# Attention products by query on 32 rows of the array, without key blocks, and identity products before the products by key

## The chip, the cores and the metric

The kernel runs on one core of a Trainium2 chip. The metric is the device time of one execution in microseconds (us), median over the runs.

## What is computed

64 sequences (B) of 128 tokens (S), width 128 (D), attend to 120 context rows each (KL) with 16 heads of 8, and a mixture of 8 experts with two experts per token follows. Both parts add to x.

```
x = x + xattn(layernorm(x), ctx, ctx, mask, Wq, bq, Wk, bk, Wv, bv, Wo, bo)
x = x + ffn(layernorm(x), Wr, W1, b1, W2, b2)

xattn:  score = einsum('bhqd,bhkd->bhqk', q, k) / sqrt(8)
        score = where(mask, -1e30, score)
        out   = softmax(score) @ v, heads joined, @ Wo + bo
ffn:    probs = softmax(x @ Wr.T); the two largest of 8 weigh
        gelu(x @ W1[e] + b1[e]) @ W2[e] + b2[e]
```

## The kernel before

It is one program with a stream written out by hand for each engine: SP and ACT issue DMAs, GpSimd (POOL) scatters rows, PE is TensorE, DVE is VectorE. Semaphores join them. The attention part works on chunks of two sequences (32 chunks) and is unrolled in slots: in `slot(n)` every engine does its share of several chunks at once, chunk n in the products by key, chunks n+1 and n+2 in the products by query, chunk n+3 in the projections, chunks n-1 to n-4 in what follows. All engines' `slot` functions list their steps in a fixed order, and so each engine works strictly in that order. The expert part (the loop `tiles`) begins after the last slot, at some 480 us.

Queries and keys are projected (L1189, L1190), split into a high and a low part in the type fp32r (L1012, L1013, L684), and spread by DMA from `comp` to `dense[c % 4]` (L292 to L302). A dense row has 128 partitions: four groups j of 32 rows, one for each of four heads, and along the free axis four groups g, each with 256 query columns (two sequences) and 240 key columns. Rows of a group of 32 that hold no part of a head carry constants: in the query columns the row MSK is one, so that a mask row in the key operand adds the mask to the score; the rows NHI and NLO take minus the largest score of each query.

The scores are computed twice:

- By query (`by_query`, L1249): the stationary operand is 128 query columns of dense with all 128 rows, the moving operand is a block-diagonal copy of the keys, `kb[c % 2]`, with 4 heads x 120 keys = 480 columns. One product gives the scores of four heads for 128 queries. DVE takes the maximum over the keys (`best`, L695). There are eight such products in a chunk, into two banks of PSUM (`wide`) in turn. The maxima are transposed (`turn_maxima`, L1287), negated and split (L702, L704), and written by DMA into the rows NHI and NLO of the query blocks (`maxima`, L327).
- By key (`by_key`, L1261): the stationary operand is 120 key columns of dense, the moving operand the block-diagonal copy of the queries `qb[c % 2]`, 4 x 128 = 512 columns. The exponential (ACT, L997) reads it from two banks (`scores`) in turn, with the mask as a bias of each key (`mcol`). Then follow the 16 products with the values (`weigh`, L1276), on all rows and 32 columns of the array each; the heads are copied (L1029) and transposed (L1216), divided (L668), transposed (L1229) and projected (L1237).

The block-diagonal copies are DMAs of four blocks each: `query_blocks` (L319) on SP's queue, a slot ahead of their use, and `key_blocks` (L1069) on ACT's queue, after the exponentials of t = 0 and 1 in the slot and ahead of `take_heads`, `take_rows` and `take_x`. `key_blocks` waits until the dense rows have landed (`dn_in`). `mask_rows` (L309) on SP writes the mask row of kb and waits for the first of the key blocks (`kfirst`). Both copies lie in memory that is cleared once at the start: kb by DVE (L878, L908), qb by ACT (`clear`). The expert part reuses kb and qb for weights.

## Time and profile before

| | us |
|---|---|
| median of 3 runs | 844.66 |
| lowest, highest | 834.1, 855.23 |
| the profiled execution | 847.77 |
| its span in the profile | 846.0 |
| attention part, first to last transposed maxima | 33.8 to 447.8 |

The profiled execution's time is 1.8 us above its span, for what lies around it. Busy times say how long an engine had an instruction in work; matmuls overlap each other, so on PE the chain of waits tells better what each adds. "issue" is time in which the profile shows nothing that was waited for.

### The profile page before, as it was taken

What the parts mean: (1) busy time and instruction counts of PE and PEld (TensorE: products, weight loads), DVE (VectorE), ACT (ScalarE), POOL (GpSimd) and SP (SyncE); (2) the same over time, 40 slices, a digit from 0 to 9 for tenths busy, and PEclk for the clock granted to TensorE, in tenths of its full rate; (3) what the DMA queues carried; (4) which work ended last, traced back from release to release, by engine and by line L of the source; (5) the groups of instructions that cost most, each with busy time, mean ns of one, the idle gap of its engine ahead of it and who ended that gap; (6) DMA issues with size and microseconds to landing.
All of it is one profiled execution on the core that took longest, in us unless ns stands there. A gap on an engine that the chain in (4) does not pass through costs nothing.

```text
span 846.0 us, 18252 instructions
## 1 busy us (share of the span) xinstructions
PE 658.2 (78%) x4964; PEld 494.5 (58%) x4964; DVE 554.3 (66%) x1813; ACT 528.3 (62%) x1060; POOL 492.4 (58%) x892
## 2 busy tenths in 40 slices
PE   1787888878888988888888376998888898988500
PEld 0455666656566666666565255876776686766400
DVE  4556778867877778687875454666555565646436
ACT  3466776856776767667776265877666676858300
POOL 8233376665757666676768642675654565665710
PEclk9879999989998999999999578999999999999855
DMA  4756667666766576566751368876666756664069
GB/s 139 211 165 188 209 209 238 187 186 191 231 193 190 190 229 209 171 204 179 222 167 61 94 217 258 253 234 196 205 195 192 220 181 195 215 207 132 10 243 352
DMA packets 118905, 164.24 MB, mean 194 GB/s; under 512 B 22479, under 2 KB 77286, under 8 KB 118823
## 3 DMA queue, kind: packets, MB, share of 16 engines
q1 hardware_dynamic: 88711, 126.14, 48.3%
q10 hardware_dynamic: 21024, 20.06, 8.3%
q0 software_dynamic: 9088, 17.07, 6.4%
q8 instruction: 36, 0.59, 0.3%
q14 instruction: 46, 0.38, 0.1%
HBM read 73.07 MB, written 33.92 MB: 126 GB/s over the span
## 4 chain that ended last, share of the span: by engine, by line
PE 53%; issue 13%; ACT 8%; DMA 7%; POOL 6%; ACTq 6%; DVE 4%; SPq 2%; another core or an unknown queue 1%; POOLq 0%; DVEq 0%
ACTq L1069 5%; PE bank L1261 5%; PE bank L1249 4%; PE bank L1276 4%; PE bank L1429 4%; PE bank L1427 4%; PE bank L1428 4%; PE bank L1412 3%; PE bank L1415 3%; PE bank L1413 3%; DMA qb<-yd 3%; PE bank L1189 3%; PE bank L1216 2%; ACT pt L997 2%; POOL xd L538 2%
## 5 line engine op out<-in xcount | busy, mean ns | idle before, releaser
L638 POOL DMA_INDIRECT yd<-vs,idt x156 | 159.5, 1022 | 129.4 <-DVE vs L949 84.5
L538 POOL DMA_INDIRECT xd<-rows,posi x128 | 128.9, 1007 | 104.9 <-DVE posi L800 75.2
L935 DVE TENSOR_TENSOR qb<-hid,qb 128x512 fp32r<-128x512 f32 x156 | 108.3, 694 | 105.6 <-ACT hid L1143 68.4
L695 DVE TENSOR_REDUCE mx<-bank 128x4 f32<-128x480 f32 x256 | 159.7, 649 | 26.4 <-PE bank L1249 19.6
L997 ACT ACTIVATE pt<-bank,mcol 120x512 f32<-120x512 f32 x256 | 168.5, 692 | 10.2 <-PE bank L1261 10.1
L1140 ACT ACTIVATE qb<-bank,btile 128x512 fp32r<-128x512 f32 x156 | 109.1, 699 | 80.1 <-PE bank L1429 55.7
L1261 PE MATMUL bank<-qb,dense 128*120 128x512 f32 x256 | 103.6, 470 | 11.6 <-issue 4.5
L1143 ACT ACTIVATE hid<-bank,btile 128x512 f32<-128x512 f32 x156 | 108.8, 697 | 0.0
L1029 ACT ACTIVATE ots<-bank 128x512 f32<-128x512 f32 x64 | 38.2, 598 | 102.5 <-PE bank L1276 36.8
L1249 PE MATMUL bank<-kb,dense 128*128 128x480 f32 x256 | 88.8, 428 | 7.2 <-DVE mx L695 3.4
L1276 PE MATMUL bank<-pt,vs 120*32 120x128 f32 x2048 | 72.8, 282 | 1.5 <-issue 1.4
L1276 PEld LDWEIGHTS bank<-pt,vs 120*32 120x32 f32 x2048 | 54.1, 112 | 23.5 <-issue 16.3
L1249 PEld LDWEIGHTS bank<-kb,dense 128*128 128x128 f32 x256 | 46.4, 201 | 27.6 <-DVE mx L695 10.0
L1261 PEld LDWEIGHTS bank<-qb,dense 128*120 128x120 f32 x256 | 42.4, 195 | 25.2 <-issue 13.4
L665 DVE RECIPROCAL rden<-bank 128x16 f32<-128x16 f32 x64 | 16.2, 254 | 48.7 <-PE bank L1216 48.5
L1216 PE MATMUL bank<-ident,ots 128*128 128x128 f32 x256 | 43.9, 299 | 2.9 <-ACT x2s L1077 2.9
L1427 PE MATMUL bank<-kb 128*128 128x512 f32 x80 | 33.8, 422 | 10.3 <-issue 6.9
L548 POOL TENSOR_TENSOR y<-ve,minus_half 128x4 f32<-128x4 f32 x38 | 39.6, 1042 | 3.2
L1427 PE MATMUL bank<-kb,qb 128*128 128x512 f32 x76 | 32.5, 427 | 11.3 <-DVE kb L901 11.3
L1216 PEld LDWEIGHTS bank<-ident,ots 128*128 128x128 f32 x256 | 35.2, 163 | 7.3 <-ACT ots L1029 3.6
L1229 PE MATMUL bank<-ident,on 128*128 128x128 f32 x64 | 19.1, 299 | 24.4 <-ACT xT L1003 19.2
L1412 PE MATMUL bank<-qb 128*128 128x512 f32 x76 | 34.7, 457 | 2.2 <-ACT qb L1140 2.2
(169 smaller groups left out, 1559.7 us busy)
## 6 DMA issues: line engine op xcount, KB each, us to landing
kb<-wd SPq DMA_DIRECT2D x40, 512.0 KB
qb<-wd SPq DMA_DIRECT2D x38, 512.0 KB
qb<-dense SPq DMA_DIRECT2D x128, 128.0 KB
dense<-comp SPq DMA_DIRECT2D x64, 248.0 KB
kb<-dense ACTq DMA_DIRECT2D x128, 120.0 KB
rows<-xd SPq DMA_DIRECT2D x39, 264.0 KB
wd<-wsp SPq DMA_DIRECT2D x16, 512.0 KB
qb<-yd SPq DMA_DIRECT2D x16, 512.0 KB, 6.0
```

Of the source, the lines that this page charges most:

```text
L538: g.indirect_dma_start(xd, bass.IndirectOffsetOnAxis(ap=posi[r % 4][:, bk:bk + 1], axis=0), rows[r % 4][:, bk // 2, bk % 2, :], None, boun ...
L638: g.indirect_dma_start(yd, bass.IndirectOffsetOnAxis(ap=idt[k][:, j:j + 1], axis=0), yrow[p.parity][:, j, :], None, bounds_check=2 * NTOK ...
L695: v.tensor_reduce(mx[c % 2][:, :, gg, b], wide[m % 2][:, 0:J * KL].rearrange("p (j k) -> p j k", j=J), op=ALU.max, axis=AX.X).then_inc(w_f ...
L935: v.tensor_tensor(hhl[:, 1, c, :], hid[:, c % 2, :], hhl[:, 0, c, :], ALU.subtract).then_inc(h_lo, 1)
L997: a.activation(pt[i % NP][:].rearrange("p j q -> p (j q)"), scores[t % 2][0:KL, :], ACT.Exp, bias=mcol[:, 2 * c + t // G:2 * c + t // G + ...
L1140: a.activation(hhl[:, 0, c, :], bank[c][:, :], ACT.Gelu, bias=bias).then_inc(h_hi, 1)
L1143: a.activation(hid[:, c % 2, :], bank[c][:, :], ACT.Gelu, bias=bias).then_inc(h_val, 1)
L1216: last = t_.transpose(small[0][:, g * P:(g + 1) * P], ots[w % 2][:, g, :], ident[:, :])
L1249: t_.matmul(wide[m % 2][:, 0:J * KL].rearrange("p (j k) -> p j k", j=J), dense[c % ND][:, g, b * S:(b + 1) * S], kb[c % 2][:, :, g, b * KL ...
L1261: t_.matmul(scores[t % 2][0:KL, :].rearrange("p (j q) -> p j q", j=J), dense[c % ND][:, g, N2 + b * KL:N2 + (b + 1) * KL], qb[c % 2][:, :, ...
L1276: last = t_.matmul(heads[R * j:R * j + R, g * S:(g + 1) * S], vs[c % 2][:, b, G * g + j, :], pt[(4 * w + g) % NP][:, j, :], start=True, st ...
L1427: t_.matmul(bank[c][:, :], w[:, 0, 0, cs], xh, start=True, stop=False)
```

## The change

- `kb`, `key_blocks`, its semaphores and its clearing are gone. `by_query` takes both operands straight from dense: for each head group j a product on the 32 rows of j, 128 query columns stationary and 120 key columns moving. 32 products a chunk stand for eight. They come in four groups of eight: two values of j in turn, each with its own bank, for the four g. A group waits until both banks are free and signals each bank at its last product.
- A bank now holds the four g of one j (it held the four j of one g); `best` writes the maxima accordingly.
- The mask row goes into the key columns of dense (`mask_rows`), in all four groups of 32 rows; it is in both products now, so the exponential has no bias and the transposed mask isn't loaded. The constant rows are set up by other values of MSK, NLO, NHI.
- `qb` has three buffers and not two. `query_blocks` is issued one slot earlier and now waits for `dn_in` itself; `mask_rows` stands ahead of it.
- Ahead of every even product by key there is a product of the identity with itself, plain fp32, 256 columns, into the first bank of `scores`, which the product by key then overwrites.
- The expert part's four weight tiles lie in qb[1] and qb[2]; the split x has a buffer of its own.

```diff
-        NHI, NLO, MSK = 3, 7, 11
+        MSK, NLO, NHI = 11, 15, 31
...
             def mask_rows(c):
+                if c < ND:
+                    sp.wait_ge(dense_set, 2 * (c + 1))
+                else:
+                    sp.wait_ge(b_full, 8 * (c - ND + 1))
                 if c == 0:
                     sp.wait_ge(mask_dram, 16)
-                sp.wait_ge(kfirst[c % 2], 16 * (c // 2 + 1))
-                sp.dma_start(kb[c % 2][MSK:MSK + 1]...
+                sp.dma_start(dense[c % ND][MSK::R, :, N2:NK]...
...
             def query_blocks(c):
-                if c < 2:
-                    sp.wait_ge(qb_zero, c + 1)
+                if c < NB:
+                    sp.wait_ge(qb_zero[c], 1)
                 else:
-                    sp.wait_ge(b_full, 8 * (c - 1))
+                    sp.wait_ge(b_full, 8 * (c - NB + 1))
+                sp.wait_ge(dn_in[c % 2], 64 * (c // 2 + 1))
...
             def slot(n):
-                if chunk(n + 1):
-                    query_blocks(n + 1)
+                if chunk(n + 3):
+                    mask_rows(n + 3)
                 if chunk(n + 2):
-                    mask_rows(n + 2)
+                    query_blocks(n + 2)
...
-                v.tensor_reduce(mx[c % 2][:, :, gg, b], wide[m % 2][:, 0:J * KL].rearrange("p (j k) -> p j k", j=J),
+                v.tensor_reduce(mx[c % 2][:, j, :, b], wide[m % 2][:, 0:G * KL].rearrange("p (g k) -> p g k", g=G),
...
-            v.memset(flat(kb[0], "p j g n").bitcast(F32), 0.0).then_inc(kb_zero, 1)
+            v.memset(flat(qb[2], "p j g n").bitcast(F32), 0.0).then_inc(qb_zero[2], 1)
...
-                if n == -3:
-                    v.memset(flat(kb[1], "p j g n").bitcast(F32), 0.0).then_inc(kb_zero, 1)
...
-                a.activation(pt[i % NP][:].rearrange("p j q -> p (j q)"), scores[t % 2][0:KL, :], ACT.Exp,
-                             bias=mcol[:, 2 * c + t // G:2 * c + t // G + 1], scale=SCALE).then_inc(exp_done, 1)
+                a.activation(pt[i % NP][:].rearrange("p j q -> p (j q)"), scores[t % 2][0:KL, :], ACT.Exp, scale=SCALE).then_inc(exp_done, 1)
...
-            def key_blocks(c):
-
-                if c < 2:
-                    act.wait_ge(kb_zero, c + 1)
-                else:
-                    act.wait_ge(w_full, 8 * (c - 1))
-                act.wait_ge(dn_in[c % 2], 64 * (c // 2 + 1))
-                for j in range(J):
-                    act.dma_start(kb[c % 2][R * j:R * j + R, j, :, :].bitcast(F32),
-                                 dense[c % ND][R * j:R * j + R, :, N2:NK].bitcast(F32)).then_inc((kblk if j else kfirst)[c % 2], 16)
...
-            def by_query(c, u):
+            def by_query(c, p):
...
-                b, g = divmod(u, G)
-                if u == 0:
-                    pe.wait_ge(kblk[c % 2], 48 * (c // 2 + 1))
-                    pe.wait_ge(mask_row[c % 2], 16 * (c // 2 + 1))
-                m = 8 * c + u
-                if m >= 2:
-                    pe.wait_ge(w_free, m - 1)
-                t_.matmul(wide[m % 2][:, 0:J * KL].rearrange("p (j k) -> p j k", j=J), dense[c % ND][:, g, b * S:(b + 1) * S],
-                          kb[c % 2][:, :, g, b * KL:(b + 1) * KL], start=True, stop=True).then_inc(w_full, 1)
+                b, half = divmod(p, 2)
+                if p == 0:
+                    pe.wait_ge(dn_in[c % 2], 64 * (c // 2 + 1))
+                    pe.wait_ge(mask_row[c % ND], 16 * (c // ND + 1))
+                m = 8 * c + 2 * p
+                if m:
+                    pe.wait_ge(w_free, m)
+                for g in range(G):
+                    for k in range(2):
+                        j = 2 * half + k
+                        last = t_.matmul(wide[k][:, g * KL:(g + 1) * KL], dense[c % ND][R * j:R * j + R, g, b * S:(b + 1) * S],
+                                         dense[c % ND][R * j:R * j + R, g, N2 + b * KL:N2 + (b + 1) * KL], start=True, stop=True, tile_position=(R * j, 0))
+                        if g == G - 1:
+                            last.then_inc(w_full, 1)
...
             def by_key(c, t):
...
+                if t % 2 == 0:
+                    t_.matmul(scores[0][:, 0:2 * P].rearrange("p (a n) -> p a n", a=2), ident[:, :],
+                              ident[:, :].rearrange("p (a n) -> p a n", a=1).to_broadcast([P, 2, P]), start=True, stop=True)
```

On PE, around the first products by key of a slot in the middle of the attention part, the order before is this (each row is an instruction with what it writes and reads; L1261 by key, L1249 by query, L1276 with the values, L1237 the output projection):

```order
L1309 MATMUL bank<-wrT,x2s 128x8 x2
L1216 MATMUL bank<-ident,ots 128x128 x4
L1261 MATMUL bank<-qb,dense 120x512 x2
L1237 MATMUL bank<-wraw,onT 128x128
L1249 MATMUL bank<-kb,dense 128x480 x2
L1276 MATMUL bank<-pt,vs 32x128 x16
```

and after the change (L1252 is the identity product, L1254 by key, L1237 by query, L1221 the projection, L1269 with the values):

```order
L1302 MATMUL bank<-wrT,x2s 128x8 x2
L1200 MATMUL bank<-ident,ots 128x128 x4
L1252 MATMUL bank<-ident 128x256
L1254 MATMUL bank<-qb,dense 120x512 x2
L1221 MATMUL bank<-wraw,onT 128x128
L1237 MATMUL bank<-dense 128x120 x8
L1269 MATMUL bank<-pt,vs 32x128 x16
```

Nothing has changed places; one instruction is added and two have become eight.

On ACT, at the beginning of a slot, the order before is this (L997 exponentials, L1059 of the router, L1029 the heads, L1077 and L1003 what PE transposed):

```order
L997 ACTIVATE pt<-bank,mcol 120x512
L1059 ACTIVATE tope<-topd 128x16
L997 ACTIVATE pt<-bank,mcol 120x512
L1069 DMA kb<-dense 32x4x240 x4
L1029 ACTIVATE ots<-bank 128x512
L1077 ACTIVATE x2s<-bank 128x256
L1003 ACTIVATE xT<-bank 128x256
```

and after the change:

```order
L995 ACTIVATE pt<-bank 120x512
L1056 ACTIVATE tope<-topd 128x16
L995 ACTIVATE pt<-bank 120x512
L1026 ACTIVATE ots<-bank 128x512
L1063 ACTIVATE x2s<-bank 128x256
L1000 ACTIVATE xT<-bank 128x256
```

The four DMA issues are gone from between the exponential and the heads.

On SP, a slot before the change (L319 query blocks, L309 mask row, L292 to L302 dense rows, L327 maxima):

```order
L319 DMA qb<-dense 32x4x256 x4
L309 DMA kb<-maskd 1x16x240
L292 DMA dense<-comp 32x4x256
L294 DMA dense<-comp 32x4x240
L327 DMA qb<-negm 1x32x128 x2
L300 DMA dense<-comp 32x4x496
L302 DMA dense<-comp 32x4x496
```

and after it:

```order
L309 DMA dense<-maskd 4x4x240
L320 DMA qb<-dense 32x4x256 x4
L289 DMA dense<-comp 32x4x256
L291 DMA dense<-comp 32x4x240
L328 DMA qb<-negm 1x32x128 x2
L297 DMA dense<-comp 32x4x496
L299 DMA dense<-comp 32x4x496
```

The mask row has moved ahead of the query blocks, and both now belong to the chunk after the one they served before.

## Rows read from the trace of the kernel before

**Rows 1.** The page, part 1: busy us, share of the span, instructions

```profile
PE 658.2 (78%) x4964; PEld 494.5 (58%) x4964; DVE 554.3 (66%) x1813; ACT 528.3 (62%) x1060; POOL 492.4 (58%) x892
```

**Rows 2.** The line L1287: ns least/median/most, first and last start in us

```profile
L1287 PE MATMUL bank<-ident,mx x32: 270/273/421, 33.8 to 447.8; 128*32 128x128 f32 x32
```

**Rows 3.** Busy us of each engine between 60 and 450 us

```profile
core 0: us, PE busy (x) PEld busy (x) DVE busy (x) ACT busy (x) POOL busy (x), PEclk, DMA share, GB/s
60.00:450.00 390.00, 334.56 (x3373) 242.22 (x3372) 299.88 (x1283) 274.86 (x626) 247.86 (x505) 0.96 0.66 196
```

**Rows 4.** The chain of waits, 236 to 268 us: start us, length us, what

```profile
239.53 0.41 PE bank L1309 x4
...
252.74 1.90 issue
254.64 0.72 PE bank L1261 x2
255.37 0.22 PE bank L1237 x2
255.59 0.43 PE bank L1249 x2
256.02 1.64 PE bank L1276 x32
...
260.62 0.60 PE bank L1189 x2
261.22 0.41 PE bank L1190 x2
...
262.07 0.46 PE bank L1261 x2
...
263.07 1.01 PE bank L1276 x32
...
264.50 0.44 PE bank L1201 x4
...
266.10 0.49 PE bank L1309 x4
266.59 0.49 PE bank L1216 x4
...
267.14 0.84 PE bank L1261 x2
```

**Rows 5.** The chain between 60 and 450 us: shares by line, longest pieces

```profile
by line: issue 13.0%; PE bank L1261 10.7%; ACTq L1069 10.2%; PE bank L1276 9.4%; PE bank L1249 8.6%; PE bank L1216 5.1%; ACT pt L997 4.9%; PE bank L1189 4.5%; PE bank L1237 4.1%; PE bank L1190 3.3%; PE bank L1201 3.0%; ACT xn L1043 2.6%; DM
...
132.59 5.05 DMA kb<-dense
146.88 4.75 DMA kb<-dense
```

**Rows 6.** Instructions of ACT in order of time, 225 to 232 us

```profile
227.43 3.27 ACTq L1069 DMA_DIRECT2D kb<-dense  x3
230.80 0.60 ACT L1029 ACTIVATE ots<-bank 128x512 f32<-128x512 f32 x1 [3.12 <-issue]
```

**Rows 7.** The line L1069: ns least/median/most, first and last start

```profile
L1069 ACTq DMA_DIRECT2D kb<-dense x128: 592/632/1714, 18.8 to 433.4; - x128
```

**Rows 8.** Groups between 60 and 450 us: busy us, mean ns, idle before

```profile
L695 DVE TENSOR_REDUCE mx<-bank 128x4 f32<-128x480 f32 x232 | 145.1, 648 | 21.3 <-PE bank L1249 14.5 <-issue 5.7 <-remote 0.5
...
L1249 PEld LDWEIGHTS bank<-kb,dense 128*128 128x128 f32 x232 | 40.3, 194 | 19.6 <-DMA kb<-dense 5.6 <-issue 3.8 <-DVE mx L695 3.7
...
L1309 PEld LDWEIGHTS bank<-wrT,x2s 128*128 128x128 f32 x108 | 14.1, 190 | 0.9
```

**Rows 9.** PE's waits between 60 and 450 us: total, times, longest

```profile
PE bank L1229 <- ACT xT L1003: 17.2, 15, 1.9
...
PE bank L1229 <- issue: 4.1, 6, 1.1
```

**Rows 10.** The chain of waits, 10 to 24 us

```profile
16.25 3.26 DVE kb L908
...
19.54 0.62 ACTq L1069
```

More of the change, by code:

```diff
@@ L90, in moe_attention @@
         dense = [sb(f"dense{k}", [P, G, NK], F32R) for k in range(ND)]
-        qb = [sb(f"qb{k}", [P, J, G, N2], F32R) for k in range(2)]
-        kb = [sb(f"kb{k}", [P, J, G, K2], F32R) for k in range(2)]
+        qb = [sb(f"qb{k}", [P, J, G, N2], F32R) for k in range(NB)]
         vs_all = [sb(f"vs{k}", [P, 2, H, R]) for k in range(2)]
@@ L104, in moe_attention @@
         bias_qk = sb("bias_qk", [P, 2])
-        ones_k = sb("ones_k", [P, 1])
+        pad_q = sb("pad_q", [P, 1])
+        pad_k = [sb(f"pad_k{i}", [P, 1]) for i in range(3)]
         masku = sb("masku", [B, KL], mask.dtype)
@@ L201, in moe_attention @@
         w_in, w_in2, wqk_in, bias_in = (sem(k) for k in ("w_in", "w_in2", "wqk_in", "bias_in"))
-        dense_set, kb_zero, qb_zero, pad_set = sem("dense_set"), sem("kb_zero"), sem("qb_zero"), sem("pad_set")
+        dense_set, qb_zero, pad_set = sem("dense_set"), [sem(f"qb_zero{k}") for k in range(NB)], sem("pad_set")
         x_in, ctx_in = four("x_in"), [sem(f"ctx_in{k}") for k in range(NC)]
-        mask_in, mask_f, mask_dram, mcol_done = sem("mask_in"), sem("mask_f"), sem("mask_dram"), sem("mcol_done")
-        mask_row = two("mask_row")
+        mask_in, mask_f, mask_dram = sem("mask_in"), sem("mask_f"), sem("mask_dram")
+        mask_row = four("mask_row")
         ident_done, bo_done, half_done, vs_zero = sem("ident_done"), sem("bo_done"), sem("half_done"), sem("vs_zero")
@@ L211, in moe_attention @@
         w_full, w_free = sem("w_full"), sem("w_free")
-        dn_in, qblk, kblk, kfirst, mrow = two("dn_in"), two("qblk"), two("kblk"), two("kfirst"), two("mrow")
+        dn_in, qblk, mrow = two("dn_in"), [sem(f"qblk{k}") for k in range(NB)], two("mrow")
         v_full, v_taken = sem("v_full"), sem("v_taken")
@@ L977, in _, with clear @@
             a = nc.scalar
[L980 to L981 removed]
+            def clear(k):
+                a.activation(flat(qb[k], "p j g n"), ident[:, P - 1:P].to_broadcast([P, J * G * N2]), ACT.Copy, scale=0.0).then_inc(qb_zero[k], 1)
             for k, w in ((0, Wq), (1, Wk)):
```

68 lines of the change are left out of this document (28 added, 40 removed).

## The prediction

> **What bounds the kernel now.** I read the busy times first [rows 1]: no engine is full (PE 78%, DVE 66%, ACT 62%), and the matmul part, the first 450 us, differs from the expert part behind it, so I cut there. Of the change, everything lies in the attention part. The transposes of the maxima (L1287, one in a slot) start at 33.8 us for the first chunk and at 447.8 us for the last [rows 2]: 31 slots in 414 us, 13.36 us each. That period is what the change can move. In it PE is busy 334.6 us of 390, DVE 299.9, ACT 274.9, at a granted clock of 0.96 [rows 3].
>
> A busy PE says little, since records of matmuls overlap. What an instruction really adds is in the chain of waits, where each has only its own step [rows 4]. At full clock: two products by key 0.46 us, two by query 0.43, the 16 value products (32 records) 1.01, a pair of 128-column plain fp32 records 0.22, and so on. A slot holds four pairs by key (1.84), four by query (1.74), twice the value products (2.02), twice L1216 (0.93) and L1237 (0.44), and once L1189 and L1190 (0.84 without the start in L1189's 0.60), L1201 (0.44) and L1309 (0.45). The small ones, L1296, L1175, L1229, L1287 and L1319 to L1322, come to some 0.9 us at the 0.11 us a record that L1216 and L1237 show. Together that is 9.6 us of PE work. The other 3.8 us are waits and the slower pace behind them: in [rows 4] the chain stands 1.90 us before L1261, and the value products after it take 1.64 us and not 1.01.
>
> What PE waits for is in the chain's shares [rows 5]. ACTq L1069 has 10.2% of 390 us, 39.8 us or 1.36 us in a slot: the four DMA issues of the key blocks hold the ACT queue, and heads, rows and xT, which PE waits for, stand behind them. The timeline shows it [rows 6]: three of the issues from 227.43 to 230.70, and ots (L1029) only at 230.80 after 3.12 us of idle ACT. Two landings of key blocks, 5.05 and 4.75 us, are the longest pieces there [rows 5], another 0.34 us in a slot.
>
> **The change part by part.** (1) Key blocks go. Their 128 issues of 0.63 us [rows 7] leave ACT's queue: 2.5 us in a slot. ACT's busy 274.9 us over 29.2 slots is 9.4 us, with the issues 11.9, just under a short slot, as the 12.5 us from 254.64 to 267.14 in [rows 4]; without them 9.4. I take 1.36 + 0.34 = 1.7 us off the period. The 15.7 MB that they moved also go; I price that at nothing, since the landings that I have counted are their own, and it can only shorten the wait for qb<-negm.
>
> (2) Products by query. Eight of 480 columns (0.43 us a pair, 1.74 us in all) become 32 of 120 columns on 32 rows, still with 128 stationary columns each. No row shows such a product, so I bound it. From below: 216 ns for 480 columns is 54 ns for 120, and no more if everything but the columns hides: 1.7 us, no change. From above, where the load sets the pace: L1309 streams only 8 columns behind a 128-column load and takes 0.41 to 0.49 us for four records, 0.103 to 0.122 us each [rows 4]: 3.3 to 3.9 us. Its load lasts 190 ns, that of L1249 194 ns [rows 8], so the load of the fp32r operand is of the same kind. Beyond that, if a short fp32r product streamed like plain fp32: L1190 takes 0.41 us for two records of 240 columns, so 0.205 us for 120 columns: 6.6 us. The nearest row for products on part of the array is L1276: 32 records of 128 columns in 1.01 us, 32 ns each, where L1237 takes 110 ns for a record of as many columns; there four positions of the array overlap 3.5 times. The new products alternate between two positions of rows (two banks). If both load and stream overlapped the pace would be 0.103/2 = 0.052, if nothing did 0.103. I take 0.07: 2.24 us, that is +0.5 us in a slot.
>
> A rule speaks against this. The Trainium skill, page "TensorE: Matmul & The Clock Gate", section "LDWEIGHTS (loading the stationary operand)", says that a load costs by its columns and not by its rows, 32x128 as much as 128x128, and gives 107 ns by its formula. By that the 32 loads would be an estimated 3.4 us and the slot 1.2 us longer than with my value. L1309's 0.103 agrees with the figure; that fewer rows don't help is shown by no row here. The skill's page "TensorEngine Tiling (Array Packing)", section "Key Properties", says that different tiles can load and multiply in parallel, which is the lower end, but also that a change of tiling mode drains the engine; the kernel would then pay eight more such changes in a slot, which no row here prices.
>
> (3) Identity products. Four in a slot, plain fp32, 256 columns, into the first bank of scores ahead of every even product by key. L1190, the same type with 240 columns, takes 0.41 us, so 256 take 0.43 (L1189's 0.60 has a start in it): 4 x 0.43 = 1.72 us. They wait for what the product by key behind them waits for, so they can't fill its wait; they stand before it on PE, and the exponential behind them starts 0.43 us later.
>
> (4) Waits and queues. A group of eight products now needs both banks of wide free, and gives both at its end; the two maxima (648 ns each [rows 8]) then run one after the other. The next group is over 2 us away, and DVE has 299.9/29.2 = 10.3 us of work in a slot, so I price this at nothing; were the cover gone, it would be one maximum, 0.65 us, in each of four groups. On SP the mask rows and the query blocks come a slot earlier and now wait for the landing of the dense rows; behind them stand the loads and the dense rows of the next chunk. Before, SP waited there for kfirst, a landing after that of the dense rows, so nothing is later.
>
> (5) Hidden part. Of the 3.8 us, 2.1 remain after (1). Some of these are waits that more PE work covers: the last DMA of maxima, and L1229's wait for xT, 17.2 + 4.1 us in the window [rows 9], 0.73 a slot. I let 0.7 us be hidden.
>
> (6) Start. One 3.26 us memset of kb stands in the chain at 16.25 us and three issues of 0.62 behind it [rows 10]; the other memset becomes one of qb, 0.2 us longer. 3.26 + 1.86 - 0.2 = 4.9, say -5 us.
>
> Sum: 13.36 - 1.7 + 0.5 + 1.72 - 0.7 = 13.2 us, 0.2 less than before. Over 31 slots -6, with the start -11. The expert part, its weight tiles now in qb, stays. From the profiled execution's 847.8 us this gives 837. The median of the three runs is 844.7, 3 us lower, inside their own spread of 834 to 855, so I leave it at 837.
>
> **The rivals.**
> A. The two positions overlap fully and PE's waits close further: 54 ns, +0.0 for (2), 1.0 hidden. 13.36 - 1.7 + 1.72 - 1.0 = 12.4 us, -30 and -5: 813 us. For it: L1276's overlap, and the short slots of 12.5 us, in which ACT was nearly full. Against it: 120 columns are too few to cover a load, and 32 positions of columns are not positions of rows.
> B. Loads set the pace, the slower side. Place: the 32 products by query on PE; price 0.103 to 0.122 us each, +1.6 to +2.1 us in a slot for (2). 13.36 - 1.7 + 1.72 + 1.6 - 0.7 = 14.3, +28 - 5: 870 us, and 886 with 0.122. It decides from 0.095 us per product on. For it: L1309. Against it: 8 columns are not alternating rows.
> C. Short fp32r products run as plain fp32 without overlap: 0.205 each, +4.8 in a slot, 17.8 us with 0.4 hidden: 980 us. For it only the bound.
> D. The waits are replaced by others and nothing is hidden (the waits called issue have 13.0% of the chain [rows 5] and I can't name them): 13.36 - 1.7 + 0.5 + 1.72 = 13.9, +16 - 5: 859 us, no measurable change.
> A clock that falls, because the products on 32 rows or the idle time count for less, would show as B does, with a lower granted clock; the identity products stand against it, and 0.96 now says there is little to gain.
>
> **How the numbers follow.** Forecast 0.33 (its own range 826 to 850), A 0.28, D 0.10, B 0.23, C 0.06. Below 808 I see nothing; of B's tail and C some 0.09 lies above 885: range 808 to 885. Faster by over 2%, below 828, is A and a little of the forecast: 0.34. Slower by over 2%, above 862, is B and C and the edge of D: 0.30. Within 2%, about what this kernel's measurement can tell from nothing: 0.36.
>
> **What would show it.** Right: no ACTq time in the chain; ots right behind the exponential; eight products by query in the chain at about 0.56 us; identity pairs at 0.43; L1280 (the maxima's transposes) 13.2 us apart; the first one before 29 us. Eight products at 0.85 us or more are B, at 1.6 C, at 0.43 A. I am wrong in the waits if PE idle per slot stays over 2 us, and in the clock if it falls below 0.93 between 60 and 450 us.

## The result: 9.8% slower, and the profile after

| | before | after |
|---|---|---|
| median of the paired runs | 846.1 us (4) | 922.38 us (4) |
| lowest, highest | 834.1, 855.23 | 917.95, 924.8 |
| ratio, 95% interval | | 1.098 (1.084 to 1.112) |
| span of the profiled execution | 846.0 | 921.4 |
| first to last transposed maxima | 33.8 to 447.8 | 31.6 to 523.1 |
| a slot (31 of them) | 13.36 us | 15.85 us |

Executions of one kernel fall into a fast and a slow state, and a ratio given with an interval compares the fast ones alone, so it isn't the quotient of the two medians.

The time came in where the change is. The transposes of the maxima, L1280 now, answer to [rows 2]:

```profile
L1280 PE MATMUL bank<-ident,mx x32: 270/272/421, 31.6 to 523.1; 128*32 128x128 f32 x32
```

31 slots take 491.5 us, 77.5 more than before. The span grew by 75.4, so the expert part behind them is unchanged: 398 us from the last transpose to the end, in both. The page's first part [rows 1]:

```profile
PE 737.6 (80%) x5988; PEld 579.0 (63%) x5988; DVE 554.0 (60%) x1813; ACT 521.2 (57%) x1060; POOL 491.1 (53%) x892
```

PE has 79 us more of busy time, the others about what they had. The same window as [rows 3] says more, since the slots in it are fewer:

```profile
core 0: us, PE busy (x) PEld busy (x) DVE busy (x) ACT busy (x) POOL busy (x), PEclk, DMA share, GB/s
60.00:450.00 390.00, 344.37 (x3554) 268.69 (x3553) 252.18 (x1063) 226.80 (x528) 205.58 (x425) 0.92 0.45 138
```

DVE, ACT and POOL all have less to do in 390 us, so none of them is the bound. The granted clock has fallen from 0.96 to 0.92, and DMA from 0.66 to 0.45, so transfers aren't it either. The chain by line [rows 5]:

```profile
by line: PE bank L1237 12.1%; PE bank L1252 10.6%; PE bank L1254 9.8%; another core or an unknown queue 9.5%; issue 7.9%; PE bank L1269 6.2%; DVE mx L695 6.1%; PE bank L1200 5.7%; PE bank L1173 4.2%; PE bank L1174 4.0%; DVE stats L728 3.9%;
```

ACTq is gone, as forecast. New are DVE's maxima (L695, 6.1%) and "another core or an unknown queue" with 9.5%. The kernel runs on one core: this releaser is one that the profile can't name. 9.5% of 390 us over the 24.6 slots that fit there is 1.5 us in a slot. The chain in order of time shows where a slot goes:

```profile
251.80 0.59 PE bank L1237 x8
...
255.00 0.85 PE bank L1252 x2
...
256.60 0.59 PE bank L1237 x8
257.19 1.01 PE bank L1269 x32
...
259.05 0.43 PE bank L1252 x2
...
259.95 0.63 PE bank L1237 x8
260.58 1.21 DVE mx L695 x2
...
262.67 1.47 issue
264.14 0.29 DVE xres L677
264.44 0.07 DVE pick L748
264.51 0.48 another core or an unknown queue
...
266.51 0.66 DVE stats L728 x3
267.17 0.07 DVE taken L762
267.24 0.05 issue
267.29 0.18 PE bank L1312
```

From 250.5 to 260.6 the chain is PE alone, 10 us. Then the chain leaves PE for 6.7 us: a group of products by query ends, DVE takes both maxima (1.21), chooses and normalises, stands 1.47 us before the residual (L677) and counts, and at 267.29 PE goes on with the counting products (L1312). PE isn't idle for all of that. In its stream the counting products stand in the middle of a slot, behind two products by key, a group by query, the value products and four transposes, and it works through these until 265.96; then it stands for 1.33 us, as the timeline has it:

```profile
265.58 0.38 PE L1159 MATMUL bank<-ident,xn 128*128 128x128 f32 x2
267.29 0.18 PE L1312 MATMUL bank<-taken,tri 128*128 128x8 bf16 x1 [1.33 <-DVE taken L762]
```

The identity pair at 255.00 takes 0.85 us and not 0.43: the granted clock is 0.50 (1.2 GHz) from 252.7 to 256.1, some 2 us behind the end (250.5) of PE's wait for the counting products of the slot before.

What DVE waits for in front of L677 is in the table of waits (engine, line waited for, us in total, times, longest):

```profile
DVE mx L695 <- PE bank L1237: 58.7, 51, 2.7
...
PE bank L1312 <- DVE taken L762: 31.6, 21, 1.7
DVE xres L677 <- remote: 30.0, 16, 2.1
```

and, for one slot, in the timeline. In square brackets is the idle time before an instruction, with what ended it:

```profile
276.70 0.98 POOL L538 DMA_INDIRECT xd<-rows,posi  x1 [0.30 <-issue]
...
277.46 0.38 PE L1221 MATMUL bank<-wraw,onT 128*128 128x128 f32 x2
...
277.98 0.97 POOL L538 DMA_INDIRECT xd<-rows,posi  x1 [0.31 <-issue]
...
278.36 0.96 PE L1269 MATMUL bank<-pt,vs 120*32 120x128 f32 x22
...
279.79 0.60 PE L1269 MATMUL bank<-pt,vs 120*32 120x128 f32 x10 [0.47 <-issue]
279.82 0.29 DVE L677 TENSOR_TENSOR xres<-bank,xres 128x128 f32<-128x128 f32 x1 [1.80 <-remote]
```

L677 needs the product L1221, which ends at 277.84. L677 starts at 279.82. In the same moment PE, which had stopped in the middle of 32 value products, goes on. The signal came 2 us late; PE itself had gone on with the next products meanwhile and stood still for 0.47 us. GpSimd's indirect DMAs (L538), which scatter the rows to the experts, run closely one after another beside it. I call this a hold-up below. In the trace of semaphores one can count PE's signals that come over 1 us after the end of the last product that raises them, up to 430 us: 62 in the kernel after (the latest by 2.3 us), but 33 in the kernel before too. In the kernel after all 62 overlap an indirect DMA in work, and none comes before the first of these DMAs, at 104.6 us. No signal of DVE or ACT is over 0.8 us late. The counts are lower bounds, since the trace lacks records: between 60 and 430 us it has 687 signals for 847 signalling products before, and 663 for 707 after. The waits of the kernel before, in the same window, show where they fell:

```profile
ACT ots L1029 <- remote: 21.5, 10, 2.5
...
PE bank L1319 <- DVE taken L762: 7.5, 12, 1.3
```

behind the value products, where other work was in hand. Before, PE waited for the counting products' input (L1319 then) for 7.5 us in the window; after, for 31.6 (L1312).

### The profile page after: what moved, and what is told of

Read it like the earlier page. It is cut to its first block, busy times and chain, and to the rows that moved or that the text cites. A ratio compares the mean times of both kernels' runs of the same rounds, so it can differ in the third digit from the quotient of the medians.

```text
span 921.4 us, 20170 instructions
## 1 busy us (share of the span) xinstructions
PE 737.6 (80%) x5988; PEld 579.0 (63%) x5988; DVE 554.0 (60%) x1813; ACT 521.2 (57%) x1060; POOL 491.1 (53%) x892
## 4 chain that ended last, share of the span: by engine, by line
PE 54%; DVE 12%; issue 11%; another core or an unknown queue 7%; POOL 6%; DMA 4%; ACT 3%; SPq 2%; POOLq 0%; DVEq 0%; ACTq 0%
PE bank L1237 7%; PE bank L1252 6%; PE bank L1254 5%; PE bank L1269 3%; PE bank L1418 3%; DVE mx L695 3%; PE bank L1416 3%; PE bank L1417 3%; PE bank L1401 3%; PE bank L1200 3%; PE bank L1402 3%; PE bank L1404 3%; DMA qb<-yd 2%; PE bank L1173 2%
## 5 line engine op out<-in xcount | busy, mean ns | idle before, releaser
L695 DVE TENSOR_REDUCE mx<-bank 128x4 f32<-128x480 f32 x256 | 159.4, 647 | 89.9 <-PE bank L1237 84.8
L538 POOL DMA_INDIRECT xd<-rows,posi x128 | 128.8, 1006 | 157.0 <-DVE posi L800 127.4
L995 ACT ACTIVATE pt<-bank 120x512 f32<-120x512 f32 x256 | 144.7, 593 | 99.7 <-PE bank L1254 94.8
L1254 PE MATMUL bank<-qb,dense 128*120 128x512 f32 x256 | 111.2, 516 | 0.0
L1237 PEld LDWEIGHTS bank<-dense 32*128 32x128 f32 x1024 | 72.4, 200 | 46.5 <-issue 35.9
L1237 PE MATMUL bank<-dense 32*128 32x120 f32 x1024 | 90.5, 298 | 5.0 <-DVE mx L695 4.9
L1269 PE MATMUL bank<-pt,vs 120*32 120x128 f32 x2048 | 81.1, 279 | 15.3 <-issue 15.2
L1252 PE MATMUL bank<-ident 128*128 128x256 f32 x256 | 87.2, 426 | 3.8 <-DMA qb<-negm 3.8
L1416 PE MATMUL bank<-xThl,qb 128*128 128x512 f32 x156 | 65.3, 419 | 19.9 <-DVE xThl L903 19.9
L1401 PE MATMUL bank<-qb 128*128 128x512 f32 x156 | 70.5, 452 | 3.9 <-ACT qb L1124 3.9
L1269 PEld LDWEIGHTS bank<-pt,vs 120*32 120x32 f32 x2048 | 56.5, 110 | 26.8 <-issue 22.0
L1404 PE MATMUL bank<-qb 128*128 128x512 f32 x156 | 63.2, 405 | 1.6 <-DVE qb L935 1.6
L1418 PE MATMUL bank<-xThl,qb 128*128 128x512 f32 x156 | 63.9, 410 | 0.0
L1417 PE MATMUL bank<-xThl,qb 128*128 128x512 f32 x156 | 63.4, 406 | 0.0
L1402 PE MATMUL bank<-qb 128*128 128x512 f32 x156 | 62.9, 403 | 0.0
L1254 PEld LDWEIGHTS bank<-qb,dense 128*120 128x120 f32 x256 | 50.9, 199 | 10.1 <-ACT pt L995 0.4
L1416 PEld LDWEIGHTS bank<-xThl,qb 128*128 128x128 f32 x156 | 30.9, 198 | 29.7 <-DVE xThl L903 22.6
```

The lines of the kernel that those rows point to most:

```text
L538: g.indirect_dma_start(xd, bass.IndirectOffsetOnAxis(ap=posi[r % 4][:, bk:bk + 1], axis=0), rows[r % 4][:, bk // 2, bk % 2, :], None, boun ...
L695: v.tensor_reduce(mx[c % 2][:, j, :, b], wide[m % 2][:, 0:G * KL].rearrange("p (g k) -> p g k", g=G), op=ALU.max, axis=AX.X).then_inc(w_fr ...
L995: a.activation(pt[i % NP][:].rearrange("p j q -> p (j q)"), scores[t % 2][0:KL, :], ACT.Exp, scale=SCALE).then_inc(exp_done, 1)
L1237: last = t_.matmul(wide[k][:, g * KL:(g + 1) * KL], dense[c % ND][R * j:R * j + R, g, b * S:(b + 1) * S], dense[c % ND][R * j:R * j + R, g ...
L1252: t_.matmul(scores[0][:, 0:2 * P].rearrange("p (a n) -> p a n", a=2), ident[:, :], ident[:, :].rearrange("p (a n) -> p a n", a=1).to_broad ...
L1254: t_.matmul(scores[t % 2][0:KL, :].rearrange("p (j q) -> p j q", j=J), dense[c % ND][:, g, N2 + b * KL:N2 + (b + 1) * KL], qb[c % NB][:, : ...
```

## The experiments

Two theories. **L**: a loop. A group of products by query gives both banks at once, two maxima follow one another on DVE, the rest of DVE's chain stands behind them, and PE waits for its end with the counting products, which stand ahead of the products by key t = 2 and 3. **H**: the hold-ups beside GpSimd's indirect DMAs cost what the change lost. Beside them the identity products, SP's new order and the pace of the new products are suspects. Each group of runs below ran on one chip, beside the kernel before on the same chip; ratios are to that. The groups ran on different chips, which turned out to matter.

### First group: four parts (kernel before: 852.49 us)

**The change without its identity products.**

```diff
-                if t % 2 == 0:
-                    t_.matmul(scores[0][:, 0:2 * P]..., ident...
```

> The changed kernel without the four identity products in a slot. PE theory (the time is PE's own work, 4 x 0.43 us in 32 slots): 922 - 55 = 867 us. Loop theory (a loop over DVE's maxima and PE's counting products, and a hold-up of PE once in a slot, set the slot): the same work is on the path outside the loop, so 870 to 890. Clock theory (they are there for the clock): granted clock between 60 and 450 us falls from 0.92 below 0.85 and the time stays at 910 or more.

Measured: 915.37 us, ratio 1.085 (1.070 to 1.100), 15.96 us a slot. Without 1.7 us of PE work a slot the period doesn't move:

```profile
60.00:450.00 390.00, 343.10 (x3349) 251.82 (x3349) 252.28 (x1066) 218.30 (x526) 202.83 (x415) 0.82 0.45 138
```

The clock is 0.82 where it was 0.92, and PE is busy as long with 205 fewer products in the window. In this kernel the identity products pay for themselves by the clock, and what sets the period isn't PE's amount of work.

**The kernel before with identity products**, the same lines added to its `by_key`.

> The kernel before with the identity products alone. PE theory with nothing hidden: 846 + 55 = 901 us. With 0.7 us of 1.72 hidden in each slot, as in the prediction: 846 + 32 = 878 us. If waits hide them all: 846 to 855.

Measured: 858.13 us, ratio 1.016 (0.999 to 1.033), 13.90 us a slot, clock 0.98. Against the 13.36 us of the first result, the addition of 1.72 us costs 0.54 us a slot; the time itself isn't clear of no change. The identities don't carry 10%.

**The change with SP's query blocks at the end of its slot.**

```diff
             def slot(n):
                 if chunk(n + 3):
                     mask_rows(n + 3)
-                if chunk(n + 2):
-                    query_blocks(n + 2)
...
                 if chunk(n + 3):
                     spread_low(n + 3)
+                if chunk(n + 2):
+                    query_blocks(n + 2)
```

> The changed kernel with the query blocks issued at the end of SP's slot, away from the scatters. In the changed kernel PE's completion signals come up to 2 us late once a slot, where SP issues the query blocks and GpSimd scatters. If the query blocks' DMAs cause it, the delay goes away and with it up to 2 us in 28 slots: 865 to 880 us. If the scatters alone cause it, the delay stays where it is and the time stays at 915 to 925.

Measured: 916.73 us (906.05 to 929.19), median by median 1.075, 15.65 us a slot, clock 0.93. That is within 1% of the kernel after in the first result, and the late signals are still there: 63 up to 430 us, 34 of them with no query block in issue beside them. So neither this place in SP's order nor the query blocks make them.

**The change with the counting products moved behind the second pair by key.**

```diff
-                if chunk(n - 4):
-                    earlier(n - 4)
                 by_key(n, 2)
                 by_key(n, 3)
+                if chunk(n - 4):
+                    earlier(n - 4)
```

> The changed kernel with the counting products (earlier) on PE behind the products by key t=2 and t=3, not ahead of them. Loop theory: PE no longer stands 1.4 us for DVE's taken: -1.2 to -1.4 us in 28 slots, 883 to 890 us. PE theory (no such loop): within 1% of 922.

Measured: 866.73 us, ratio 1.023 (1.005 to 1.041), 14.02 us a slot. This one edit gives back some 7 points of the 9 to 10, more than the loop alone had been priced at (883 to 890 us); with the shorter wait the clock came back too. In the window PE is at full clock:

```profile
60.00:450.00 390.00, 362.25 (x4115) 285.80 (x4115) 288.27 (x1224) 260.20 (x607) 238.29 (x489) 1.00 0.51 158
```

and of its waits

```profile
DVE mx L695 <- PE bank L1237: 35.6, 56, 1.2
DVE xres L677 <- remote: 34.9, 19, 2.1
PEld bank L1312 <- DVE taken L762: 23.9, 23, 1.2
PE bank L1312 <- DVE taken L762: 13.8, 22, 0.7
```

PE's wait for L762 has halved (31.6 to 13.8 us), while the late signal in front of L677 is as it was: 34.9 us, 19 times. PE now has two products by key to do meanwhile. L is confirmed as the way on which the time is lost; whether H feeds it stays open here.

### Second group: the repaired kernel (kernel before: 805.47 us)

**The kernel before with the same move.**

> The kernel before with the counting products behind the products by key t=2 and t=3. In its slots PE stands some 1.0 us for DVE's taken. If the loop over DVE bounds only the changed kernel, this one stays within 1% of 846 to 852 us, since ACT with its DMA issues and the block landings are late next. If it bounds both: -1.0 us in 28 slots, 820 to 828 us.

Measured: 803.45 us, ratio 0.999 (0.995 to 1.003). The place of the counting products is worth nothing before and 6% after: the loop was not the bound before. This chip turned out to be one without hold-ups, so the kernel before with hold-ups and this move was not run; its period is 13.3 to 13.4 us with and without them.

**The counting products late and no identities.**

> The changed kernel with the counting products late and without identity products. Clock theory: PE's clock falls without them in whatever order, 0.85 or less in the window, and the 55 us of work saved are given back: 860 to 880 us. PE theory: the clock stays at 0.95 or above because the wait is gone, 867 - 55 = 812 us.

Measured: 758.36 us, ratio 0.937 (0.930 to 0.944), 12.2 us a slot. This was the first kernel that beat the one before, below both ranges that were expected, and a surprise beside the 1.023 of the first group. The waits say why:

```profile
DVE mx L695 <- PE bank L1237: 24.1, 49, 2.5
PEld bank L1309 <- DVE taken L762: 21.6, 26, 1.0
PEld bank L1237 <- DVE mx L695: 11.5, 28, 1.1
PE bank L1309 <- DVE taken L762: 10.4, 24, 0.6
```

No row says "remote". On this chip there are no hold-ups at all: no signal over 1 us late, and none in the kernel before with its move either. The kernel before is 47 us faster here than on the chip of the first group, and not by its period, which with the counting products late is the same 13.36 us (L1287 goes from 33.8 to 447.9). The rest behind the last transpose takes 356 us here and 398 in the first result: the difference lies in the expert part.

**The counting products late, and the query blocks behind SP's maxima; and the counting products late, with GpSimd's late scatters behind the root and the query blocks left where they were.** The cut shows the scatters of the second:

```diff
-                if late:
-                    scatter(n - 5, (2,))
...
-                if late:
-                    scatter(n - 5, (3,))
                 if n <= NCH + 1:
                     root(n)
+                if late:
+                    scatter(n - 5, (2, 3))
```

> As the counting-late kernel, with the query blocks issued behind the maxima in the middle of SP's slot, several us from the scatters. If the late completion signals of PE need the query blocks' issue beside the scatters, they go: up to 2 us in 28 slots, 815 to 840 us. If the scatters alone make them, they stay at the slot's start and the time at 860 to 870.

> As the counting-late kernel, with GpSimd's two late scatters of a slot moved behind the root, so that at most two stand together at the slot's start. If three scatters in a row cause PE's late signals, these shrink below 1 us or move to the middle of the slot: 820 to 850 us. If the query blocks cause them, they stay with L320: 860 to 870 us.

Measured: 778.12 us, ratio 0.963 (0.957 to 0.969), and 781.21 us, 0.967 (0.961 to 0.973). Both keep the identities and are 3 points behind the run without them; as there are no hold-ups here, neither could say anything of their cause. The periods are 12.6 and 12.7 us. At full clock (1.00 in both up to 430 us) the identities look like work that only costs, though each of the two has a move of its own beside them.

### Third group: the same kernels on a third chip (kernel before: 829.65 us)

**The kernel after again, the one with late counting products again, and the kernel before itself as a run.**

> The changed kernel once more, beside the other three on one chip: the first eight runs fell on two chips, on one of which the kernel before takes 852 and on the other 805 us, and the late completion signals of PE are seen on the first alone. If they are what made the change slow: on a chip without them within 2% of the kernel before, on one with them 8 to 10% slower. If the loop over DVE and the clock made it slow: 5% slower or more on either.

> The counting-late kernel beside it. Loop theory: 5 to 7% below the changed kernel on either chip, 14.0 us or less between the transposed maxima and a clock of 1.00 in the window.

> The kernel before, for its profile on the same chip. Late signals in some 45 places of the attention part if the chip has them, else none; 13.3 to 13.4 us between the transposed maxima either way; the expert part 40 us shorter where the kernel takes 805 us.

Measured: 908.66 us (893.99 to 912.02), median by median 1.095; 850.91 (836.96 to 852.94), 1.026; and 836.14, ratio 1.014 (1.002 to 1.026), which is the kernel before against itself. So a difference of 1.4% between single groups means nothing here. Both main results repeat, and both kernels after have late signals on this chip.

**Counting products late, query blocks behind the maxima, late scatters behind the root, and no identities.**

> The changed kernel with counting products late, query blocks behind the maxima, late scatters behind the root, and no identity products. If these add: below the 758 us (0.937 of the kernel before) of the counting-late kernel without identities, 0.92 to 0.93. If the clock falls: 0.94 to 0.96.

Measured: 841.99 us, ratio 1.023 (1.013 to 1.034), 13.8 us a slot, clock 0.93, outside both ranges that were expected, which were made from the chip without hold-ups. The hold-ups didn't go; they moved to where the scatters now stand, in the middle of the slot, 8 of the 74 late signals with no query block in issue beside them. That spoke for the scatters and against the query blocks, but only as two things seen side by side.

### Fourth group: once more, and the order of the products (kernel before: 848.33 us)

**The kernel after once more; and the eight products by query bank by bank.**

```diff
-                for g in range(G):
-                    for k in range(2):
+                for k in range(2):
+                    for g in range(G):
```

> The changed kernel once more. Two theories of its 9 to 10%: (L) a longer loop over DVE at the start of a slot, with PE's clock falling while it waits; (H) PE is held up for some 2 us beside GpSimd's scatters, as the chips 0 and 2 of the earlier runs showed and chip 6 did not. If the chip of this run has no hold-ups, L expects this kernel still 4 to 6% slower than the one before (the other runs gave 6% for the loop), H expects it within 2%. If it has them, both expect 1.08 to 1.10 and the run only ties the others to this chip.

> The changed kernel, its eight products by query ordered by bank and not in turn: four of one row position into bank 0 with its signal, then four of the next into bank 1. If the two maxima coming at once at the end of a group are what lengthens the loop, bank 0's maximum starts 0.3 us or more earlier and the period falls by 0.3 us a slot or more (15.85 to 15.5, some -10 us). If it is the alternation of two row positions that lets loads overlap, eight products take longer than 0.59 us in the chain (0.8 and more, the 0.103 us of a load each), +1 us in a slot or +30 us. If a position of rows makes no difference, 0.59 us stays.

Measured: 913.21 us (900.86 to 925.86), median by median 1.076, 16.0 us a slot, with late signals on this chip too; and 918.13 us (900.72 to 923.96), 15.9 us a slot, no difference. The chain of the second:

```profile
150.45 0.60 PE bank L1237 x8
153.81 0.60 PE bank L1237 x8
```

Four products in a row on one position of rows go at the same 75 ns as in turn. The alternation of positions buys nothing, and getting bank 0 some 0.3 us earlier shortens the loop by nothing that can be seen (15.9 against 16.0): the step "both maxima at once" is not where the loop is long.

**Counting products late, no identities, as in the second group; and that bank by bank.**

> The changed kernel with the counting products late and without identities, 0.937 of the kernel before on chip 6. If the chip has hold-ups: theory L with H as a second cost expects 0.98 to 1.03 (PE waits for held-up signals, its clock falls under 0.97 without the identities); if identities matter nowhere once the counting products stand late, 0.95 to 0.99. Without hold-ups 0.93 to 0.95 again.

> As the run before it with the eight products ordered by bank. Where PE no longer waits for DVE, only the pace of the products is left: if alternation of row positions overlaps loads, this is 20 to 30 us slower than the run before it; if not, the same within 1%.

Measured: 853.8 us (832.81 to 856.13) and 847.96 us (829.39 to 874.6), 1.006 and 1.000 of the kernel before, median by median; 13.7 and 13.5 us a slot. The kernel that won 6% on the second group's chip wins nothing here. Its wait is back, on another line:

```profile
DVE mx L695 <- PE bank L1237: 38.0, 65, 2.5
DVE mx L695 <- remote: 35.5, 18, 2.3
```

### Fifth group: plain DMAs for the indirect ones (kernel before: 846.5 us)

This takes away what H names, at its own place, in the attention part. GpSimd sends the same rows, 128 of 528 bytes each time, from the same place in its stream, but to fixed addresses:

```diff
-                    g.indirect_dma_start(xd, bass.IndirectOffsetOnAxis(ap=posi[r % 4][:, bk:bk + 1], axis=0),
-                                         rows[r % 4][:, bk // 2, bk % 2, :], None, ...
+                    e, k = (4 * r + bk) % E, (4 * r + bk) // E
+                    at = e * REGION + (P * k if k < 15 else REGION - P)
+                    g.dma_start(xd[at:at + P, :], rows[r % 4][:, bk // 2, bk % 2, :])...
```

SP also writes constants into both of the expert part's buffers, one or two DMAs a slot, so that every row holds numbers; that adds load and takes none away. The expert part then works on other rows, and the output isn't the layer's.

**In the kernel after, nothing else changed in its streams of PE, DVE and ACT.**

> The changed kernel with plain DMAs of the same rows, of the same size, on the same queue and at the same places of GpSimd's stream, to fixed rows in place of the indirect DMAs to routed rows (so what the expert part computes is not the layer; 8 MB are also written once so that all rows hold numbers). Theory H, the hold-ups of PE come with GpSimd's indirect DMAs: the late signals vanish (under 10, where 78 to 91 were) and the period falls by the 1 to 2 us a slot that the late signals take in the loop, from 15.8 to 14.0 to 14.8 us, a time of 860 to 890 us. Theory L alone, the loop over DVE is what costs: the period stays above 15.3 us and the time within 2% of the changed kernel's. If plain DMAs hold PE up as well, the late signals stay, and the cause is GpSimd's queue and not the indirection. On a chip like 6 (kernel before at 805 us) it has no late signals anyway, and its period against 15.85 then shows what the loop costs alone.

Measured: 832.55 us, ratio 1.000 (0.989 to 1.011). The maxima's transposes and the window:

```profile
L1285 PE MATMUL bank<-ident,mx x32: 270/272/421, 31.7 to 451.0; 128*32 128x128 f32 x32
```

```profile
60.00:450.00 390.00, 365.92 (x4263) 290.90 (x4262) 299.87 (x1273) 266.53 (x625) 199.65 (x507) 1.00 0.64 196
```

13.53 us a slot, 2.3 less than in the kernel after, at full clock, with the counting products where the change has them and with all identities. The fall is larger than H had expected (a slot of 14.0 to 14.8 us), and L alone had expected over 15.3. No signal of the attention part is over 1 us late, and no record of one is lacking (843 signals for 843 products between 60 and 430 us). That isn't the chip: in the expert part, whose indirect DMAs are untouched (L643), 47 signals are over 1 us late on this chip, where the second group's chip had none and the kernels before and after in the first result 63 and 76 (counted from 480 us; the 18 or 19 updates in the last 3 us of each trace, with no product near them, aren't signals of products). The line numbers here are five higher than in the kernel after; L682 is its L677:

```profile
DVE mx L700 <- PE bank L1242: 70.5, 86, 1.5
PEld bank L1317 <- DVE taken L767: 30.2, 27, 1.2
PE bank L1317 <- DVE taken L767: 23.9, 27, 0.9
```

```profile
L545 POOL DMA_DIRECT2D xd<-rows x104 | 59.5, 574 | 84.7 <-DVE posi L805 84.5
...
L682 DVE TENSOR_TENSOR xres<-bank,xres 128x128 f32<-128x128 f32 x58 | 16.1, 277 | 0.6 <-PE bank L1226 0.3
```

The 30.0 us for which L677 waited on "remote" are 0.6 us here. The loop is still there, PE waits for L767 in each slot, up to 0.9 us, but it is short enough.

How the 2.3 us divide can be worked out from the two windows of 390 us. The kernel after has 24.6 slots in its window: PE is busy for 14.0 us of each and idle for 1.85. With plain DMAs there are 28.8 slots: 12.7 busy and 0.84 idle. PE's work is the same in both, so only 1.0 us of the 2.3 is less waiting. The other 1.3 us is the same work at a granted clock of 1.00 in place of 0.92, and 0.08 of 15.85 us is indeed 1.3. More than half of what the hold-ups cost in the loop is paid in clock.

Two things go along with the exchange and limit the reading: a plain DMA occupies POOL for 574 ns where the indirect one took 1010, and the expert part, which now computes on other rows, is 21 us shorter (827.7 - 451.0 = 377 us against 398). The 2.3 us a slot, 72 us over the part, are read from the attention part alone.

**With the counting products late and no identities.**

> As the run before it, with the counting products late and without the identity products. On chip 6 that kernel with its indirect DMAs took 0.937 of the kernel before, period 12.2 us; on chip 9 0.998 to 1.006, period 13.7. Theory H expects the period of chip 6 here, 12.2 to 12.6 us, with under 10 late signals, and so some 35 to 45 us less than on chip 9. If the difference of the two chips is another one, 13.5 us or more.

Measured: 783.38 us, ratio 0.932 (0.917 to 0.947), of which some 21 us are the expert part's; 11.7 us a slot, no late signal in the attention part (48 in the expert part). That is below the 12.2 us of the chip without hold-ups, below what was expected (12.2 to 12.6), and 2 us below the same kernel in the fourth group. Beside the second group's run it also shows what a shorter DMA start on POOL is worth where neither has hold-ups: the median slot is 11.6 us with plain DMAs and 11.7 with indirect ones. The two means are further apart since in the second group's run three of the slots take about 17 us.

| us a slot | hold-ups | none |
|---|---|---|
| before | 13.36 (first result), 13.26 (third group) | 13.36 (second) |
| after | 15.85, 15.8, 16.0 | 13.53 (plain DMAs) |
| after, counting late | 14.0, 14.0 | 12.6 (with query blocks behind the maxima), 12.7 (with late scatters behind the root), both second group |
| after, counting late, no identities | 13.7 (fourth) | 12.2 (second), 11.7 (plain DMAs) |

The two theories are two halves of one. The hold-ups cost the kernel before nothing that its period shows; they fall beside other waits. They cost the kernel after 2.3 us in each slot, waiting and lost clock together: the wait for ACT's queue is gone, and the late signal now lies in the loop over DVE, for whose end PE stands. Take away either the hold-up or PE's place at the loop's end, and most of the loss goes.

## Why the prediction was wrong

The forecast was 837 us in 808 to 885; the result, 922, lies outside. Step by step:

- **(1) Key blocks, -1.7 us a slot: right in kind, the size not measured by itself.** There is no ACTq time in the chain. The slots before rows are scattered (from 105 us on) say little: the second to the fifth took 11.8 to 13.6 us against 12.5 to 13.5 before, but the first took 18.0 against 12.7.
- **(2) Products by query, 0.07 us each: right in size, wrong in reason.** Eight take 0.59 us, 74 ns each, against the 0.56 that I had given as the sign. I had argued from alternating row positions; bank by bank they go at the same pace. A load of 128 columns on 32 rows doesn't set the pace at 0.103 us as L1309 led rival B to say. By the 107 ns that the Trainium skill, page "TensorE: Matmul & The Clock Gate", section "LDWEIGHTS (loading the stationary operand)", has for a load of 128 columns, whatever its rows, eight would take an estimated 0.86 us: the trace has 0.59 and disagrees. Whether the fewer rows are the reason no run here shows.
- **(3) Identities, 4 x 0.43: right as a duration**, 0.43 a pair at full clock. What I hadn't in the sum was that without them the kernel isn't faster while PE waits (clock 0.82), and that the kernel before takes them for some 0.54 us a slot.
- **(4) Waits and queues, priced at nothing: this step failed.** I wrote that the next group is over 2 us away and DVE has room, which is true of an average slot, and looked only at the next group of products by query as the one who waits. The one who waits is the counting product in the middle of PE's slot, at the end of a chain over DVE of 6.7 us (260.58 to 267.29), with a late signal of PE in it. In the kernel before PE waited for the same step too, 12 times and 7.5 us in all; after, 21 times and 31.6 us. In the terms of the sum: PE's own steps grew as forecast, from 9.6 to 9.6 + 0.6 + 1.7 = 11.9 us, but what is not PE's steps was to fall from 3.8 to 1.4 us and stayed at 15.85 - 11.9 = 3.9. The 1.36 + 0.34 us of the key blocks went and as much came back, as waits on the loop and as a clock of 0.92 in place of 0.96. A wait that is small while others cover it isn't small when they go. My text asked what is late once ACT's queue is free only of the waits that I could name.
- **SP's new order, nothing: not contradicted.** Moving the query blocks to the end of SP's slot changed nothing (third run); the old order itself was not tried.
- **(5) 0.7 us hidden: not testable**, since the rest of the slot changed. With hold-ups gone, the slot takes 13.53 us where the sum had 13.2: steps (1) to (3) and (5) together were 0.3 us off. Nearly everything else of the miss is the hold-up in the loop with the clock that it costs, 2.3 us a slot, 72 us. Even without hold-ups the change would not have paid: 13.53 us is no less than the 13.36 before.
- **(6) Start, -5 us: -2.2** (33.8 to 31.6).
- **The rivals.** D ("waits are replaced by others", 859 us) named the right kind and had the waits called issue as its ground, but priced it at the hiding that is lost, not at a new wait. The wrong-side rival B was about the pace of the products, which was not it. Of the two signs that I had set for being wrong, the clock's came in: it fell under 0.93 (0.92). The other, PE idle over 2 us a slot, came in only by the measure of my sum (3.9 us that aren't PE's steps at full clock); by the window PE is idle for 1.85 us a slot, as before (1.90), and the rest is slower work.

Could it have been foreseen? The hold-ups stand in the trace of before, as 21.5 us of ACT waiting for "remote" on a kernel with a single core. I had not asked what a remote releaser can be on one core, and so not where those late signals would fall in the new order. The chain's "issue" rows, 13% [rows 5], which I said I couldn't name, were the place to look further.

What stays open: why PE is held up. It goes with the indirect DMAs, not with plain ones of the same bytes, and in the attention part it is there on the chips of the first, third and fourth group and not on the second's. What in an indirect DMA does it, and why one chip is free of it, no run here shows. That the plain DMA takes 0.44 us less of GpSimd each time wasn't separated from it on one chip; the median slots of 11.6 and 11.7 us in the kernel with late counting and no identities speak for 0.1 us, so the 2.3 us may hold a little of it. The kernel after, unchanged, did not run on the chip without hold-ups.

## What to carry to other kernels

When a change takes the covering waits away, look at the wait tables for every small wait that crosses engines, and follow the chain behind it to its start: that is the new bound, at its own length and not at the length of the wait it used to be. A step that another engine's whole chain feeds shouldn't stand in an in-order stream ahead of work that is ready; here two products by key ahead of it were worth 6%. And a wait on PE has two prices, the time that it takes and the clock behind it: here 1.0 and 1.3 us a slot. Fill a waiting PE with dummy work only if the waiting can't be removed, since the same identities were worth 0.1 of the clock while PE waited, and with the wait gone the kernel without them was the fastest.

## What was not expected of the hardware

- Beside GpSimd's indirect DMAs PE's signals come 1 us and more late, up to 2.3 us in the kernel after, and PE stops for about half a microsecond in the middle of a run of products; in the attention part with plain DMAs of the same size, not one signal is over 1 us late. The trace also lacks a fifth of PE's signals there in the kernel before (687 of 847), and none with plain DMAs.
- Chips differ. The kernel before took 805 us on one and 830 to 852 us on the others, and the one is the chip on which neither part has a late signal; the ratio of one and the same edit (late counting, no identities) was 0.937 there and 1.006 elsewhere.
- Products with 32 stationary rows, 128 stationary columns and 120 moving columns in fp32r go at 74 to 75 ns each, whether they take turns between two row positions or not.
- With the identity products the granted clock was 0.92, without them 0.82, at the same period.
